# Seven products instead of eight in the last two column blocks of tiles 8 to 15, sixteen-bit floats for all factors, and a new order of the calls of the first four tiles

## The reference

```python
def fake_quant(x, scale, zp):
    q = clip(round(x / scale + zp), 0, 255)
    return (q - zp) * scale

# x: (2, 1024, 2048) f32, ctx: (2, 2048, 2048) f32, one context matrix for each of the two batches
x = x + tanh(g_xattn) * matmul(fake_quant(layernorm(x)), fake_quant(ctx))
n = layernorm(x)
logits = n @ route_w.T                     # 8 experts; the best one is taken, its logit is the weight
h = n @ A[e].T                             # 16 numbers for each expert
x = x + tanh(g_ffn) * (weight * h[best]) @ Bw[best].T
```

## Time and profile before

| | |
|---|---|
| median of 3 runs | 363.45 us (363.37 to 363.67) |
| span of the profiled execution, first to last instruction | 361.7 us |
| PE busy | 333.0 us, 92% |
| DVE busy | 260.6 us, 72% |
| ACT busy | 197.4 us, 55% |
| POOL busy | 172.3 us, 48% |
| DMA | 87.63 MB, mean 242 GB/s |

### The profile page before, as it was taken

The page is one execution under the profiler, slowest core; times in us unless marked ns, Lnnn a source line. Parts: engine busy times, 40 slices in busy tenths (PEclk is TensorE's granted clock), DMA queues, the critical chain, the costliest instruction groups (busy, mean ns, idle before and its releaser), DMA issues.

```text
span 361.7 us, 5854 instructions
## 1 busy us (share of the span) xinstructions
PE 333.0 (92%) x2237; PEld 186.4 (52%) x2262; DVE 260.6 (72%) x553; ACT 197.4 (55%) x129; POOL 172.3 (48%) x199
## 2 busy tenths in 40 slices
PE   0389999999999999999998999999999999999983
PEld 0244454546756466455464546464464555465751
DVE  3855799898967896958658587945588567585853
ACT  1888489778967262747999270524062413204460
POOL 2559267431265162545999056627064441605281
PEclk9999999999999999999999999999999999999999
DMA  7999999895769998899799996666939890443956
GB/s 301 400 387 404 366 387 380 289 348 173 284 182 212 289 251 291 270 266 294 176 366 157 262 320 121 181 111 177 212 138 158 225 288 31 93 84 59 304 220 232
DMA packets 93906, 87.63 MB, mean 242 GB/s; under 512 B 71844, under 2 KB 72868, under 8 KB 89764
## 3 DMA queue, kind: packets, MB, share of 16 engines
q1 hardware_dynamic: 93856, 87.11, 79.5%
q10 hardware_dynamic: 12, 0.00, 0.0%
HBM read 52.49 MB, written 16.78 MB: 191 GB/s over the span
## 4 chain that ended last, share of the span: by engine, by line
PE 77%; DVE 8%; DMA 7%; issue 2%; ACT 2%; POOL 2%; ACTq 0%; SPq 0%; DVEq 0%
PE main L1575 46%; DMA xs<-in_x 4%; PE hp L1613 4%; PE hp L1617 4%; PE hp L1614 4%; PE outp L1575 4%; PE outp L1658 4%; PE outp L1660 3%; PE outp L1659 3%; DVE bn L971 3%; PE turn L1609 2%; DMA prow<-in_g_ffn 2%; DMA out<-xs 1%; ACT x L753 1%; PE turn L1503 1%
## 5 line engine op out<-in xcount | busy, mean ns | idle before, releaser
L1575 PE MATMUL main<-q,qa 128*128 128x512 bf16 x841 | 194.6, 380 | 5.0 <-POOL q L593 2.3
L1575 PEld LDWEIGHTS main<-q,qa 128*128 128x128 bf16 x864 | 83.2, 98 | 101.2 <-issue 2.7
L586 POOL TENSOR_TENSOR yn<-y,yn 128x2048 f16<-128x2048 f32 x13 | 53.0, 4077 | 31.7 <-ACT y L788 31.7
L735 ACT ACTIVATE c<-stage,zpc,inv 128x2048 int8<-128x2048 f32 x24 | 49.9, 2086 | 7.7 <-DMA stage<-in_ctx 4.0
L593 POOL CAST q<-c 128x2048 bf16<-128x2048 int8 x24 | 45.1, 1893 | 15.3 <-ACT c L735 14.8
L782 ACT ACTIVATE yn<-xs,sc 128x2048 f16<-128x2048 f32 x11 | 23.0, 2093 | 53.4 <-POOL sc L579 49.6
L1104 DVE SCALAR_TENSOR_TENSOR xs<-main,cc,xs 128x512 f32<-128x512 f32 x45 | 33.3, 740 | 21.7 <-PE main L1575 21.5
L574 POOL TENSOR_SCALAR ve<-mv 128x1 f32<-128x1 f32 x16 | 3.1, 191 | 84.8 <-DVE mv L1137 81.8
L1184 DVE SCALAR_TENSOR_TENSOR xs<-outp,tsc,xs 128x512 f32<-128x512 f32 x44 | 31.2, 735 | 13.6 <-PE outp L1660 13.5
L971 DVE BATCH_NORM_STATS2 bn<-xs 128x6 f32<-128x512 f32 x52 | 32.1, 680 | 10.6 <-DMA xs<-in_x 10.6
L753 ACT ACTIVATE x<-xs,sc 128x2048 int8<-128x2048 f32 x12 | 25.0, 2087 | 24.5 <-POOL sc L566 24.4
(11 more groups left out here) (132 smaller groups left out, 435.2 us busy)
## 6 DMA issues: line engine op xcount, KB each, us to landing
stage<-in_ctx SPq DMA_DIRECT2D x24, 1024.0 KB, 7.9
xs<-in_x SPq DMA_DIRECT2D x13, 1024.0 KB, 6.5
out<-xs SPq DMA_DIRECT2D x12, 1024.0 KB, 5.0
yT<-in_ctx SPq DMA_DIRECT2D x4, 1024.0 KB, 9.2
y<-in_ctx SPq DMA_DIRECT2D x4, 1024.0 KB, 10.1
c<-in_x SPq DMA_DIRECT2D x3, 1024.0 KB, 7.4
out<-c SPq DMA_DIRECT2D x3, 1024.0 KB, 7.3
c<-in_L_ffn_A SPq DMA_DIRECT2D x1, 1024.0 KB, 11.5
```

Of the source, the lines that this page charges most:

```text
L586: pool.tensor_tensor(yn[:, 1, :], y[:, :], yn[:, 0, :], ALU.subtract).then_inc(s_ylo_made, 1)
L735: act.activation(c8_of(piece), place(piece), ACT.Identity, bias=zpc[:, 1:2], scale=inv[:, 1:2])\
L1575: last = pe.matmul(bank_of(n)[:, :], q1T(t)[:, k, :], q2[:, nb, k, :], start=(k == 0), stop=(k == KC - 1))
```

## The change

From tile 8 on, tiles go in pairs (t, t+1). Blocks 0 and 1 of both are computed as before. Blocks 2 and 3 of both tiles together are a 2x2 problem: the rows are two tiles, the inner dimension has two halves of 8 chunks (HK = 8), the columns are two blocks. It is done by Winograd's form of Strassen's scheme: seven products of 8 matmuls each (`product`) in place of eight (four units of 16 matmuls). The factors are sums: on the side of x three sums of a pair in `qs` (`make_sum`, one of them made again in place, so four instructions a pair, 128x1024 f16), and on the side of the context four sums made once (`make_t1` to `make_t4`, in two halves each, eight instructions of 128x2048 f16), which lie in `c8` and in `q2`. Products m1, m6, m5, m3 accumulate in one bank (`turn0`) and m7, m4 in another (`turn1`), m2 in a main bank; each product's partial sum is added to x on DVE by `add_product`, seven additions a pair in place of four.

For this `q2`, `q1` and `qa` become f16 in place of bf16. Room is found by dropping the second half of `yn`: the low part of the second norm is written over `y`, and `norm_full(t)` now waits for the DMA transpose of tile t-1's low part. Tiles 11 and 12 have their home in `stage`. `flip_q1` of an even tile from 10 on waits for product m2 and for the fourth sum of the pair before, `flip_q1` of an odd tile for m4.

The written orders of all engines are new: for the first four tiles (loads too), and for tiles 6 to 15.

The core of the diff:

```diff
+ADDED = {1: (0, W0), 2: (0, W0), 3: (0, W0 + 1), 4: (1, W0), 5: (1, W0 + 1), 6: (1, W0), 7: (1, W0 + 1)}
...
-HOME = [0, 7, 1, 2, 3, 4, 0, 1, 2, 3, 4, 6, 7, 0, 1, 2]
+HOME = [0, 7, 1, 2, 3, 4, 0, 1, 2, 3, 4, 8, 9, 0, 1, 2]
...
+        def factor_b(i):
+
+            return {1: q2[:, W0, 0:HK, :], 2: q2[:, W0, HK:KC, :], 3: q2[:, W0 + 1, HK:KC, :], 4: c8h[2],
+                    5: c8h[1], 6: c8h[0], 7: q2[:, W0 + 1, 0:HK, :]}[i]
+
+        def factor_a(t, i):
+
+            return {1: q1T(t)[:, 0:HK, :], 2: q1T(t)[:, HK:KC, :], 3: qs[:, 1, :, :], 4: q1T(t + 1)[:, HK:KC, :],
+                    5: qs[:, 0, :, :], 6: qs[:, 1, :, :], 7: qs[:, 2, :, :]}[i]
...
             def flip_q1(t):
 
-                sp.wait_ge(s_main_done, UNIT[q1_home_before(t), NB - 1] + 1)
+                if t < TB + 2:
+                    sp.wait_ge(s_main_done, UNIT[t - 2, NB - 1] + 1)
+                elif t % 2:
+                    sp.wait_ge(s_main_done, max(UNIT[t - 2, W0 - 1], UNIT[t - 3, "m4"]) + 1)
+                else:
+                    sp.wait_ge(s_main_done, UNIT[t - 2, "m2"] + 1)
+                    sp.wait_ge(s_sum_made[3], (t - TB) // 2)
                 sp.wait_ge(s_q1_ready, t + 1)
...
+                if j == 1:
+                    if done:
+                        dve.wait_ge(s_main_done, UNIT[t - 2, "m5"] + 1)
+                    dve.tensor_tensor(qs[:, 0, :, :], low[:, 0:HK, :], low[:, HK:KC, :], ALU.add)\
+                       .then_inc(s_sum_made[0], 1)
...
+                if j == 4:
+                    dve.wait_ge(s_sum_made[1], done + 1)
+                    dve.wait_ge(s_main_done, UNIT[t, "m6"] + 1)
+                    dve.tensor_tensor(qs[:, 1, :, :], top[:, HK:KC, :], qs[:, 1, :, :], ALU.subtract)\
+                       .then_inc(s_sum_made[3], 1)
...
+            def make_t3(half):
+                dve.wait_ge(s_t1_made, half + 1)
+                s, count = widened(LATE + 2 + half)
+                dve.wait_ge(s, count)
+                dve.tensor_tensor(in_q2(LATE + half), in_q2(LATE + 2 + half), in_q2(LATE + half), ALU.subtract)\
+                   .then_inc(s_t3_made, 1)
...
+            def add_product(t, i):
+
+                n, (into, nb) = UNIT[t, f"m{i}"], block_of((t, f"m{i}"))
+                x_nb = xcol(into, nb * NW, (nb + 1) * NW)
+                dve.wait_ge(s_main_done, n + 1)
+                for u in MAINS[:n]:
+                    if block_of(u) == (into, nb):
+                        dve.wait_ge(s_main_added, UNIT[u] + 1)
+                dve.scalar_tensor_tensor(out=x_nb, in0=bank_of(n)[:, :], scalar=cc[:, :], in1=x_nb,
+                                         op0=ALU.mult, op1=ALU.add).then_inc(s_main_added, 1)
+                if COMPLETES[into, nb] == (t, f"m{i}"):
+                    dve.wait_ge(s_main_added, n + 1)
+                    bn_block(into, nb)
...
+            def product(t, i, run):
+
+                n = UNIT[t, f"m{i}"]
+                if run == 0:
+                    pe.wait_ge(s_main_added, bank_before(n) + 1)
...
+                for k in range(4 * run, 4 * run + 4):
+                    first = i in (1, 2, 7) and k == 0
+                    last = pe.matmul(bank_of(n)[:, :], factor_a(t, i)[:, k, :], factor_b(i)[:, k, :],
+                                     start=first, stop=(k == HK - 1), skip_group_check=i in (6, 5, 3, 4))
+                if run == 1:
+                    last.then_inc(s_main_done, 1)
```

More of the change, by code:

```diff
@@ L268, in build @@
         turn = [bank("turn0"), bank("turn1")]
-        turnb = [t[:, :].bitcast(bf16) for t in turn]
+        turnb = [t[:, :].bitcast(f16) for t in turn]
         hp = bank("hp")
@@ L1340, in _ @@
             add_main(5, 2)
-            add_main(5, 3)
+            add_experts(3, 0)
+            tile_terms(6, range(NB))
             take_q1T(6, 0)
-            stats2_sum(5)
-            tile_terms(6)
-            add_experts(3, 0)
             take_q1T(6, 1)
-            stats1(7)
             add_experts(3, 1)
@@ L1350, in _ @@
             add_experts(3, 3)
+            add_main(5, 3)
+            stats2_sum(5)
+            add_experts(4, 0)
+            add_experts(4, 1)
+            stats1(7)
+            tile_terms(7, range(NB))
             add_main(6, 0)
+            add_experts(4, 2)
+            add_experts(4, 3)
             add_main(6, 1)
+            stats1(8)
+            take_q1T(7, 0)
             add_main(6, 2)
+            take_q1T(7, 1)
             add_main(6, 3)
             stats2_sum(6)
-            take_q1T(7, 0)
@@ L1388, in _ @@
-            add_main(9, 1)
+            add_main(7, 3)
+            add_main(8, 0)
+            add_experts(6, 0)
+            make_sum(8, 3)
+            stats2_sum(7)
+            make_sum(8, 1)
+            make_t1(0)
+            add_main(8, 1)
+            add_experts(6, 1)
+            make_sum(8, 2)
+            make_t1(1)
+            late_terms(8)
+            make_t3(0)
+            late_terms(9)
+            make_t3(1)
+            make_t2(0)
+            add_main(9, 0)
+            stats1(10)
@@ L1978, in _ @@
+            main(12, 0, 3)
+            product(12, 1, 0)
+            main(12, 1, 0)
+            main(12, 1, 1)
             expert_product(8, 2)
@@ L2028, in _ @@
-            main(13, 3, 3)
+            main(13, 0, 1)
+            expert_product(9, 2)
+            product(12, 6, 0)
+            product(12, 6, 1)
+            expert_product(9, 3)
+            product(12, 7, 0)
+            product(12, 7, 1)
+            turn_wh(10)
+            main(13, 1, 0)
+            main(13, 0, 2)
+            expert_product(10, 0)
+            main(13, 1, 1)
+            product(12, 4, 0)
+            product(12, 5, 0)
+            product(12, 5, 1)
+            expert_product(10, 1)
```

1046 lines of the change are left out of this document (571 added, 475 removed).

## The result

The change made the kernel slower: 369.97 us (median of 4 runs, 368.85 to 370.90) against 363.41 for the kernel before on the same chip, a ratio of 1.0173 with a 95% interval of 1.0149 to 1.0198. I had forecast 358.8 with a range up to 364.5. The profiled execution, the slowest of the four, took 370.9 with a span of 369.1, that is 7.4 more than the span of before and 12.1 more than the 357.0 of my sum.

What follows compares the result with a forecast made beforehand. PE was taken to bound the kernel from about 28 to 340 us. Terms -6.9 + 2.6 + 1.0 + 1.5 - 1.4 - 1.5 = -4.7 us took 363.45 to 358.8, range 354.5 to 364.5.

Steps and rivals of the forecast that it cites:

- The first four tiles: Start of kernel: new order wins back PE idle time despite a later first main; -1.5 us, bounds -4 and +2.2.
- Rival D: Start of kernel: first main 2.2 us later and nothing regained; 362.5 us, chance 0.12.
- POOL beside DVE: 24 new DVE operations: POOL and DVE can shut each other out; +1.5 us, bounds 0 and 6.
- Rival C: DVE and POOL shut each other out, notably low rows of tile 7 against T1 to T2; 363.3 us, chance 0.20.
- The transposes: Pairs: tile 10's 4.8 us transpose counted in the first pair's stall; those of tiles 12 and 14 hidden by PE work.
- The matmuls: Four pairs on PE, each 56 matmuls in place of 64, f16 costing nothing against bf16; -6.9 us.
- The sums: DVE's new f16 sums at the lower bounds, 0.675 us for 1024 elements and 1.23 for 2048.
- rival B: DVE's sums run at one element a cycle, the upper bounds; 370 us, chance 0.11.
- The first pair: Eight context sums fall among its products, so PE waits for DVE and tile 10's transpose; +2.6 us, between 1 and 12.
- The later pairs: Three later pairs: banks pass between products only through an addition, a third of a us each; +1.0 us, between 0 and 3.
- The gap at 193.87: PE's 1.4 us gap goes because the new order moves DVE's expert addition and statistics; -1.4 us, bounds -1.4 and 0.

Runs made afterwards that it cites:

- e4_quarters: Changed kernel with POOL's subtraction for the low rows of tile 7 cut into four 128x512 parts; 1.0055 of the kernel before.
- p2_order_alone: Kernel before with only the new order of the first four tiles on all five engines, none of the seven products; 1.0059 of the kernel before.
- p1_products_alone: Changed kernel with the seven products, but the first four tiles in the order of the kernel before; 1.0072 of the kernel before.
- c8: Changed kernel with column_sums calls spread and POOL's subtraction for tile 7's low rows waiting for the first half of T2; 0.9964 of the kernel before.
- t1_bodies_out: Changed kernel with the bodies of three column_sums calls left out, their conditional blocks kept; 359.56 us, 0.9870 of the kernel before.
- e1: Changed kernel with the four column_sums calls in a row in TensorE's list spread between products; 1.0061 of the kernel before.
- e2: Changed kernel with the addition that frees main(9,0)'s bank ahead of T2 in DVE's list; 1.0071 of the kernel before.
- e3: Changed kernel with 24 unused 128x256 matmuls added ahead of the first pair's second product, where TensorE waits; 1.0136 of the kernel before.
- t2: Changed kernel with turn_router ahead of the three last column_sums calls in TensorE's list; 1.0117 of the kernel before.
- c4b: Changed kernel with column_sums spread, tile 7's subtraction in quarters, and the addition freeing main(9,0)'s bank ahead of T2; 0.9976 of the kernel before.

## Why the prediction was wrong

The direction was wrong, and three terms failed, with one mechanism that is missing from all of them.

**The first four tiles, -1.5, is the first step that failed.** I weighed PE's idle time and the DMA queues, said that the router's transposes leave a crowded place, and priced nothing of what TensorE's own list does at the new one. There four blocks passed over leave PE without work for 2.74 us, and with the slow clock behind it this cost 6.0 us in the profiled execution. As a term the new order came to +2.1 in the kernel before, and to some +3.7 in the changed one (1.0173 less 1.0072, on two chips), where I had -1.5 and +2.2 as upper bound. Without the gap the -1.5 was near: 1.1 us more of PE's work done by 84 us. The first main came at 19.95 (forecast 19); PE was then 2.8 us of busy time behind the kernel before at 20 us, and 0.8 at 40 us. Rival D had this term lose, by another mechanism.

**POOL beside DVE, +1.5, is the second.** Rival C named the place, the low rows of tile 7 against T1 to T2, and its price on DVE, +3.4; measured 3.9, which cost PE 6.5 us in the profiled execution and 4.3 by the median of `e4_quarters`. I gave it 0.20, because the one row that I had showed POOL waiting for DVE, never the reverse, and I spread a mean over 24 sums where it was one meeting of two long instructions. The Trainium skill (SBUF — State Buffer, "SBUF: two separate sides") says that whichever starts first holds the other off for the whole instruction. I had cited it and not drawn the consequence that a fraction of a microsecond decides between 0 and 3.9. The traces agree with it: the sum ends 1.08 us after POOL's end where POOL was first, and takes 1.21 us where the sum was.

**The transposes, put at nothing but for tile 10, is the third, and smaller.** Behind 84 us the trace of the kernel before has no wait of PE for a DMA, nor has `p2_order_alone`. PE waits 3.7 us in the changed kernel and 3.6 in `p1_products_alone`, so these waits come with the products: for q1 of a tile (1.35 at 192.99, 0.80 at 283.72) and for rows of the second norm (0.92 at 344.01). What in the products makes them late is open. They show in the kernels with both gaps mended, which stayed at 0.994 to 0.998, that is 361.2 to 362.6 us beside 363.41, and not at 358.8: in `c8` all of PE's waits behind 84 us are 5.8 us, where the sum had 3.6 for the pairs. Only `t1_bodies_out`, with 4.0 us, reached the sum, a span of 357.5 where it said 357.0, and that took the luck told above.

**Missing in every step: the clock.** I wrote that a wait costs its full length. Behind these two gaps it cost more, 6.0 for 2.74 and 6.5 for 3.83 in the changed kernel. With it rival C would have stood at about 363.3 + 2.7 = 366, not at 363.3.

**Right.** The matmuls, -6.9: 32 fewer, at the old pace in f16, twelve in 2.76 us, (2.76 - 0.38) / 11 = 0.216 each. The sums at 0.67 and 1.21 us: rival B, 370, came close to the measured time for a reason that is not in it, and would have been the wrong lesson. The first pair, +2.6, at the lower of its bounds: without the gap (`t1_bodies_out`) it waited 0.85 before product (6,0) and 0.19 at tile 10, so 1.0. The later pairs, +1.0: 0.80 and 0.16 in the changed kernel, near in size, but the 0.80 is a transpose of q1 and not an addition that a bank waits for. The gap at 193.87, -1.4: it went, but in the changed kernel a wait of 1.35 for the transpose of tile 8 took its place at 192.99; `t1_bodies_out` has neither.

## What to carry to other kernels

Where a long POOL instruction and a long DVE one may meet, look up which can start first and by how much, and order the two with a semaphore rather than average over them. Price a gap of PE of 2 us or more at 1.4 to 2.3 times its length, which is what such gaps cost here where the clock fell behind them. Work put into it kept the clock up here, though the time gained was not clear of the noise. Spread conditional blocks with long bodies between products, and time a mended kernel beside its parent: most of the waits taken away one by one here came back at the next product.

## What the runs showed of the hardware

- A DVE sum of two f16 operands waited for a POOL subtraction to end, and then took 1.08 us more, in six kernels alike (the changed one, `e1`, `e2`, `e3`, `p1`, `t2`). In the order reversed (`t1`) the sum took the 1.21 us that it takes alone and POOL's 4.33 us; with the two apart (`c8`) POOL's took 4.07.
- The clock did not follow the length of a gap alone: it fell to 0.50 after 2.74 and after 2.15 us near 43 us (the changed kernel, `e2_bank_first`) and after 1.75 in `e3_fill`, and it stayed at 1.00 after 2.01 in `t2_router_first` at the same place, after 2.19 at 19.95 in the changed kernel and after 1.83 in `c4b`. (The profiled execution of `t2_router_first` was the fastest of four, 365.42 us at a mean clock of 0.992; the others took 367.6 to 369.1 at 0.984 to 0.988 and probably did lose the clock there.) How long it stayed low differed too: about 7 us behind the second gap of the changed kernel, 3 behind a gap as long in `e1` and `p1`.
- Four blocks of 16 matmuls that are passed over left PE idle for 1.75 to 2.74 us at 42 us (five kernels), and not at all at 211 us of another.
